# State-space scan kernel: the C row spread by fp32 transposes instead of bf16 parts, and two reorderings

## The reference, cut to what matters

```python
x_dbl = einsum('bkdl,kcd->bkcl', xs, x_proj_w)          # 8 dt rows, 16 B rows, 16 C rows
dts = softplus(einsum('bkrl,kdr->bkdl', dts, dt_projs_w) + dt_projs_b)
def step(h, inp):
    u, dt, Bl, Cl = inp
    dA = exp(dt[..., None] * A)
    h = h * dA + (dt * u)[..., None] * Bl[:, :, None, :]
    y = einsum('bkdn,bkn->bkd', h, Cl)
    return (h, y)
```

## Time and profile before

| | |
|---|---|
| median of 3 runs (lowest to highest) | 27172.97 us (27160.68 to 27182.06) |
| the profiled execution, its own time | 27187.59 us |
| its span in the trace | 27185.8 us |
| busy share of the span: DVE, ACT, POOL, PE | 93%, 87%, 86%, 80% |
| first layer and setup of the second (0 to about 3230 us) | not touched but for the setup |

### The profile page before, as it was taken

One profiled execution on the slowest core, in us unless ns is written; L12 is line 12 of the kernel. 1 busy time (PEld: TensorE's weight loads), 2 busy tenths in 40 slices (PEclk: granted clock), 3 DMA queues, 4 the chain that ended last, 5 costly groups with the idle time before them and its releaser, 6 DMA issues.

```text
span 27185.8 us, 494791 instructions
## 1 busy us (share of the span) xinstructions
PE 21719.7 (80%) x145198; PEld 16495.5 (61%) x145198; DVE 25255.5 (93%) x23743; ACT 23580.4 (87%) x48522; POOL 23338.1 (86%) x10372
## 2 busy tenths in 40 slices
PE   5888588888888888888888888888888888888887
PEld 1666366666666666666666666666666666666666
DVE  7777599999999999999999999999999999999999
ACT  2677499999999999999999999999999999999998
POOL 4000299999999999999999999999999999999999
PEclk6999799999999999999999999999999999999999
DMA  4111433333333333333333333333333333333333
GB/s 149 49 47 47 147 109 108 108 108 110 107 111 108 108 109 107 109 108 109 108 109 106 110 108 109 109 107 110 109 108 108 108 108 108 107 108 109 108 109 97
DMA packets 2189148, 2868.62 MB, mean 106 GB/s; under 512 B 695002, under 2 KB 964858, under 8 KB 2177786
## 3 DMA queue, kind: packets, MB, share of 16 engines
q1 hardware_dynamic: 2181978, 2803.33, 33.7%
q10 hardware_dynamic: 4608, 33.82, 0.3%
HBM read 2667.01 MB, written 169.74 MB: 104 GB/s over the span
## 4 chain that ended last, share of the span: by engine, by line
ACT 34%; PE 23%; issue 17%; DVE 11%; POOL 3%; ACTq 1%; DVEq 0%; POOLq 0%
DVE hst L1535 9%; ACT dbT L1424 8%; ACT dAs L1402 8%; PE yps L1240 7%; ACT dA L1402 6%; PE misc L1141 5%; PE dbx L1225 5%; ACT vab L1357 2%; PE misc L1177 2%; PE misc L1160 2%; POOL hc L1612 2%; DVE hc L1543 1%; ACT dbx L1402 1%; ACT vab L1343 1%; POOL dbu L1598 1%
## 5 line engine op out<-in xcount | busy, mean ns | idle before, releaser
L1598 POOL TENSOR_TENSOR dbu<-dtu,bb 128x1024 f32<-128x1024 f32 x4096 | 9699.4, 2375 | 867.0 <-DVE hst L1535 859.8
L1535 DVE TENSOR_TENSOR_SCAN hst<-dA,dbu 128x1024 f32<-128x1024 f32 x4096 | 9348.4, 2282 | 494.9 <-ACT dA L1402 417.8
L1612 POOL TENSOR_TENSOR hc<-hst,cc 128x1024 f32<-128x1024 f32 x4096 | 9734.0, 2376 | 4.9 <-DVE hst L1535 4.5
L1240 PE MATMUL yps<-ident,hc 128*128 128x128 f32 x65536 | 8781.6, 280 | 348.2 <-POOL hc L1612 343.5
L1240 PEld LDWEIGHTS yps<-ident,hc 128*128 128x128 f32 x65536 | 7809.8, 145 | 1479.9 <-issue 797.3
L1535 DVE TENSOR_TENSOR_SCAN hst<-dAs,dbx 128x1024 f32<-128x1024 f32 x3584 | 8118.4, 2265 | 102.2 <-ACT dAs L1402 51.7
L1225 PE MATMUL dbx<-ident,dbT 128*128 128x128 f32 x28672 | 4061.3, 287 | 3024.4 <-DVE hst L1535 2713.6
L1424 ACT ACTIVATE dbT<-dtuT,bT 128x256 f32<-128x256 f32 x14336 | 6124.6, 495 | 18.2
L1225 PEld LDWEIGHTS dbx<-ident,dbT 128*128 128x128 f32 x28672 | 3309.8, 146 | 4385.5 <-DVE hst L1535 3366.5
L1402 ACT ACTIVATE dA<-dtv,aneg 128x508 f32<-128x508 f32 x8192 | 5289.2, 678 | 371.6 <-DVE hst L1535 365.8
L1402 ACT ACTIVATE dAs<-dtv,aneg 128x508 f32<-128x508 f32 x7168 | 4741.1, 710 | 385.1 <-DVE hst L1535 385.0
(11 more groups left out here) (187 smaller groups left out, 25487.1 us busy)
## 6 DMA issues: line engine op xcount, KB each, us to landing
bb<-l_bscr SPq DMA_DIRECT2D x1024, 1024.0 KB, 5.7
cc<-l_bscr SPq DMA_DIRECT2D x1024, 1024.0 KB, 5.5
bx<-l_bscr SPq DMA_DIRECT2D x1024, 256.0 KB, 6.1
xg<-xgp SPq DMA_DIRECT2D x512, 85.0 KB, 2.3
xgp<-xb ACTq DMA_DIRECT2D x32, 1032.0 KB, 9.4
xt<-in_x_dram SPq DMA_DIRECT2D x128, 256.0 KB, 2.8
l_xnT<-xo SPq DMA_DIRECT2D x128, 256.0 KB, 2.0
xn<-l_xnT SPq DMA_DIRECT2D x256, 128.0 KB, 2.1
```

Of the source, the lines that this page charges most:

```text
L1240: mm = pe.matmul(yps[:, p, f * P:(f + 1) * P], hc[:, u % HB, f * 512 + p * P:f * 512 + (p + 1) * P], ident[:], is_transpose=True, start=fi ...
L1535: nc.vector.tensor_tensor_scan(hst[:, v % 4, way], decays.rearrange("p f c -> p (f c)")[:, way], inputs.rearrange("p f c -> p (f c)")[:, way],
L1598: nc.gpsimd.tensor_tensor(to, dtu[:, step % 2], row.unsqueeze(1).to_broadcast([P, 2, 512]), ALU.mult).then_inc(s_inp, 1)
L1612: nc.gpsimd.tensor_tensor(hc[:, v % HB].rearrange("p (f c) -> p f c", f=2), hst[:, v % 4].rearrange("p (f c) -> p f c", f=2), row.unsqueez ...
```

## The change

1. C by transposes. `side` with k = 0 turned the 128 rows of `xdbl` into columns already, for B. Now ACT copies the C columns as well (`bcT`, 32 columns in each of four positions of 128, before 16). `spread_c` makes four fp32 transposes, each of one column of `bcT` repeated 128 times, in place of one bf16 matmul. The casts (L1336, L1340), the matmuls of `split` (L1170), the constants `selc` and `nident` and the copies of the C rows in the projection's weights go. The x projection has 40 output rows in place of 104.
2. PE's order. In a step pair of DVE's kind the spread of C for u+2 now stands ahead of `total(u)`, also where it stood behind. Where POOL has the even product (u % 16 = 10), `total(u-1)` and `side` now stand ahead of the next `fill`. For u = 58 `total(u)` stays ahead of the spread, since no job stands at 58.
3. ACT's order. Decay 44 moves from the start of the pair u = 42 to right behind the Silus of u = 40, ahead of `scale(45)`.

The core of the diff:

```diff
-                        nc.scalar.copy(xdbl[0:104, j[2] % 2], misc[0:104, :])
-                        wait(act, s_cb, n * (NCD // 4) - NCD // 4)
-                        nc.scalar.copy(part[:, j[2] % 2], misc[0:96, :]).then_inc(s_me, 1)
-                    elif what == "split":
-
-                        r = 64 if j[3] == 1 else 32
-                        nc.scalar.copy(part[0:r, j[2] % 2], misc[0:r, :]).then_inc(s_me, 1)
+                        nc.scalar.copy(xdbl[0:DTR + 8, j[2] % 2], misc[0:DTR + 8, :]).then_inc(s_me, 1)
...
-                def spread_c(ph, u):
+                def spread_c(u):
 
                     step = u // NST
-                    if u % NST == 0:
-                        pe.wait_ge(s_me, ph.misc(("own" if step else "pre", "split", step, 2)))
-                    pe.matmul(cps[:, :], selc[:, u % NST], part[:, u // NST % 2], start=True, stop=True).then_inc(s_cb, 1)
+                    for p in range(4):
+                        mm = pe.transpose(cps[:, p * P:(p + 1) * P],
+                                          bcT[:, step % 2, p, u % NST:u % NST + 1].to_broadcast([P, P]), ident[:])
+                    mm.then_inc(s_cb, 1)
...
+                        if c_pool(u):
+                            total_odd()
+                            if ph.has(c):
+                                side(c[1], c[2], at(ph, c[0]))
+                            fill_next()
+                        else:
+                            fill_next()
+                            total_odd()
                             pe.wait_ge(s_hc, b * NCD + (c_dve_of(u) + 1))
-                        c = SIDE.get(u)
-                        if ph.has(c):
-                            side(c[1], c[2], at(ph, c[0]))
+                            if ph.has(c):
+                                side(c[1], c[2], at(ph, c[0]))
                         job_of(ph, u)
-                        early = ph.has(c) and u in JOBS
-                        if not early:
+                        if ph.has(c) and u not in JOBS:
                             total(u, b)
...
+                            spread_next()
+                        else:
+                            spread_next()
                             total(u, b)
...
                         if u + 2 < UN:
-                            decay(ph, u + 2, b)
+                            if u != SILU_AT + 2:
+                                decay(ph, u + 2, b)
...
                         if u == SILU_AT:
                             silus(ph, not last, True, b)
+                            decay(ph, u + 4, b)
```

More of the change, by code:

```diff
@@ L665, in layer1 @@
     UN = 4 * NST
+    DTR = 2 * NST
     HB = 4
@@ L709, in layer1 @@
         pbwd = sb("pbwd", [P, 2, P])
-        selc = sb("selc", [96, NST, P], BF16)
         wconv = sb("wconv", [P, 2, 9, P])
         wz = sb("wz", [P, 2, P])
-        wx = sb("wx", [P, 4, 2, 104])
-        wdt = sb("wdt", [104, 4, 2, P])
+        wx = sb("wx", [P, 4, 2, DTR + 8])
+        wdt = sb("wdt", [DTR + 8, 4, 2, P])
         wo = sb("wo", [P, 2, P])
@@ L743, in layer1 @@
         dtuT = sb("dtuT", [P, 2, 4, 256])
[L744 removed]
+        bcT = sb("bcT", [P, 2, 4, DTR])
         dbT = sb("dbT", [P, 2, 4, 256])
@@ L804, in _ @@
                         (pbwd[:], T["pbwd"].rearrange("o l q -> l o q")),
-                        (selF, T["selc"]),
                     ]
@@ L831, in _ @@
                     last.then_inc(s_scaled, 1)
-                    nc.vector.tensor_copy(selc[:], selF)
                     nc.vector.tensor_scalar(dtc[:], dtb[:], -1.0, 20.0, ALU.mult, ALU.add)
@@ L1159, in job @@
                         for f in range(2):
-                            mm = pe.matmul(misc[0:104, :], wx[:, KS[step], f], xs[:, KS[step] % 2, f],
+                            mm = pe.matmul(misc[0:DTR + 8, :], wx[:, KS[step], f], xs[:, KS[step] % 2, f],
                                            start=(f == 0), stop=(f == 1))
@@ L1265, in _ @@
                 pe.wait_ge(s_ce, 3)
-                spread_c(PRO, 0)
+                spread_c(0)
                 fill(1, 0)
@@ L1272, in body @@
                     for u in range(0, UN, 2):
-                        if turned(u + 3) and u + 3 < UN:
-                            fill(u + 3, b)
-                        elif u + 3 > UN and not last:
-                            fill(u + 3 - UN, b + 1)
-                        if u:
-                            total(u - 1, b)
-                        elif not (isinstance(b, int) and b == 0):
-                            total(UN - 1, b - 1)
-                        if not c_pool(u):
+                        c = SIDE.get(u)
@@ new lines, in fill_next, with total_odd @@
+                        def fill_next():
+                            if u + 3 > UN:
+                                if not last:
+                                    fill(u + 3 - UN, b + 1)
+                            elif turned(u + 3):
+                                fill(u + 3, b)
+                        def total_odd():
+                            if u:
+                                total(u - 1, b)
+                            elif not (isinstance(b, int) and b == 0):
+                                total(UN - 1, b - 1)
@@ new lines, in spread_next @@
+                        def spread_next():
+                            if ph.has(c):
+                                pe.wait_ge(s_ce, (at(ph, c[0]) * 4 + c[1]) * 3 + (c[2] + 1))
+                            if u + 2 < UN and not c_pool(u + 2):
+                                spread_c(u + 2)
+                            elif u + 2 == UN and not last:
+                                spread_c(0)
+                        if c_pool(u):
[6 more added lines that the diff above has]
+                            total_odd()
@@ L1289, in body @@
                             total(u, b)
-                        if ph.has(c):
-                            pe.wait_ge(s_ce, (at(ph, c[0]) * 4 + c[1]) * 3 + (c[2] + 1))
-                        if u + 2 < UN and not c_pool(u + 2):
-                            spread_c(ph, u + 2)
-                        elif u + 2 == UN and not last:
-                            spread_c(ph, 0)
-                        if early:
+                            spread_next()
+                        else:
+                            spread_next()
@@ L1411, in side @@
                     if k == 0:
-                        nc.scalar.copy(bT[:, step % 2], cps[:].rearrange("p (w n) -> p w n", w=4)[:, :, NST:2 * NST]).then_inc(s_ce, 1)
+                        nc.scalar.copy(bcT[:, step % 2], cps[:].rearrange("p (w n) -> p w n", w=4)[:, :, 0:DTR]).then_inc(s_ce, 1)
                     else:
@@ L1423, in scale @@
                     for p in blocks:
-                        last = nc.scalar.mul(dbT[:, turned_of(v) % 2, p], dtuT[:, step % 2, p], bT[:, step % 2, p, st:st + 1])
+                        last = nc.scalar.mul(dbT[:, turned_of(v) % 2, p], dtuT[:, step % 2, p], bcT[:, step % 2, p, NST + st:NST + st + 1])
                     if blocks[-1] == 3:
@@ L1685, in shape_constants @@
     pbwd = np.stack([np.ascontiguousarray(pfwd[:, o * P:(o + 1) * P].T) for o in range(2)])
-    selc = np.zeros((96, 16, P), np.float32)
-    for part in range(3):
-        for n in range(16):
-            selc[32 * part + n, n, :] = 1.0
     group = np.kron(np.eye(P // 4), np.full((4, 4), 0.25)).astype(np.float32)
-    return {"group": group, "ident": np.eye(P, dtype=np.float32), "pfwd": pfwd, "pbwd": pbwd, "selc": selc}
+    return {"group": group, "ident": np.eye(P, dtype=np.float32), "pfwd": pfwd, "pbwd": pbwd}
 def build(nc, given, out, N):
@@ L1698, in build @@
     second = {name[len("L1_conv_"):]: ap for name, ap in given.items() if name.startswith("L1_conv_")}
-    consts = {name: given[name] for name in ("ident", "group", "pfwd", "pbwd", "selc")}
+    consts = {name: given[name] for name in ("ident", "group", "pfwd", "pbwd")}
     layer0(nc, {**first, **consts, "l0_ln_w": first["ln_w"], "l0_ln_b": first["ln_b"], "x": given["x"], "x1T": x1T, "xgp": xgp}, N)
```

34 lines of the change are left out of this document (12 added, 22 removed).

## The result

The changed kernel takes 27276.53 us (median of 6 runs, 27273.56 to 27285.15). The kernel before takes 27175.58 us in its 6 runs, so the ratio is 1.0038, with an interval of 1.0028 to 1.0048. It is 0.38% slower, where 0.95% faster was forecast.

The account below looks back on a forecast made before the run. DVE and POOL, waiting for each other, were taken as the bound. Gains of 1.94 us per block times 127, 246 us, plus about 8 us in setup and prologue led to 26915 us, 0.95% faster; 8-in-10 range 26730 to 27070.

Parts of the forecast that it names:

- Steps 16 and 21: Product of step 16 and scan 21: earlier side copy and two fewer ACT casts gain 0.85 us per block together.
- Step 60: Product of step 60: total and side ahead of the fill end DVE's stall, leaving POOL's input 62 late; gain 0.55 us per block.
- Step 2: Product of step 2: its spread goes ahead of total 0 and decay 4 loses one cast; gain 0.25 us per block.
- Step 55: Softplus at step 55: ACT loses three casts between steps 49 and 52, so the vab waits go; gain 0.29 us per block.
- The Silu stall: DVE's 3.17 us wait at scan 44: cut up into waits at scan 44, scan 45 and the product of 44; gain 0.
- The rival that the stall really goes: At scan 44: the wait really disappears, gaining 1.0 us more per block, to POOL's limit, about 26790 us; chance 0.17.
- Spread: PE's four transposes replacing one matmul: +0.22 us each time, 28 times a block, 6.2 us of PE time.
- The sum: Whole kernel: gains of 1.94 us per block over 127 blocks, 246 us, plus about 8 us outside them; 26915 us.
- The setup's term: Setup and prologue: a load, a cast of selc, 16 small copies and first splits go; about 8 us gained, an estimate.
- PE's low clock: Rival, where PE has only transposes (step 55 to 0): low clock makes PE the bound, 27300 us; chance 0.04.
- the four terms of this forecast: Per-block gains: 0.85 us at steps 16 and 21, 0.55 at step 60, 0.25 at step 2, 0.29 at step 55.

## Why the prediction was wrong

**Steps 16 and 21 (forecast 0.85 us).** Right: 0.68 us in the changed kernel, and as much with the loads moved. Step 16 kept 0.60 us of its stall, not 0.3.

**Step 60 (forecast 0.55).** Right in kind, 0.70 us, and scan 62 now waits for POOL's input, as forecast:

```profile
14662.15 2.26 DVE L1534 TENSOR_TENSOR_SCAN hst<-dA,dbu 128x1024 f32<-128x1024 f32 x1
...
14668.12 2.29 DVE L1534 TENSOR_TENSOR_SCAN hst<-dA,dbu 128x1024 f32<-128x1024 f32 x1 [0.42 <-ACT dAs L1399]
```

```profile
14665.58 4.75 POOL L1597 TENSOR_TENSOR dbu<-dtu,bb 128x1024 f32<-128x1024 f32 x2
```

The view names `dAs` as what ended this wait (in 115 blocks), but scan 62 does not read `dAs`, and the program has it wait only for decay 62, which had ended 1.26 us earlier in the mean. POOL's input 62, the first of the two products in the row, ended 0.12 us ahead of scan 62 in each of blocks 4 to 123.

**What failed is the question behind this step.** Of the stall at 60 I asked who is late next among the engines, and stopped at POOL. I did not ask what else is timed by the same steps. SP sends the loads of the next block when POOL is through with its inputs, and that stands between the stall and the block's end. So the forecast put the block's start, scan 0 to 1, at nothing. Without the stall DVE reaches the branch 0.76 us sooner after these loads (scan 0 stands 6.35 us behind them in the mean of before, 5.59 now), and scan 1 comes 0.46 us later. The view of the earlier trace rows even had the sign of it, in a group of scans that I left out of my list of DVE's waits:

```profile
DVE hst L1535 <- issue: 49.3, 95, 1.0
```

It is now 101.8 us.

**Step 2 (forecast 0.25).** Wrong in the changed kernel, 0.35 us lost, and right with the loads moved, 0.32 gained. I had read this wait as one of PE's order, and it was one of PE's clock. In the kernel before (blocks 4 to 123) the clock falls in step 1 in 60 blocks, which are the half with the wait (4.72 us from scan 3 to 4); in the other 60 it falls just before the block begins, and the distance is 3.29 us, without a wait. In the changed kernel it falls in step 1 in 98.

**Step 55 (forecast 0.29).** 0.07 lost, and 0.33 gained with the loads moved. This term, too, named the wrong cause. In the kernel before the vab wait at step 55 is there in 60 blocks, exactly those in which PE's clock falls at step 54; without that fall the distance is 3.95 us. In the kernel with ACT's new order alone, which keeps every cast, the clock never falls at step 54 and the same 0.33 us are gained. In the changed kernel it still falls there in 50 blocks, which then take 4.92 us. The casts had no part in this wait. Where they do count is scan 21: 0.48 us there, and 0.50 with the spread alone.

**The Silu stall (forecast 0, bounds -0.1 and +1.0).** The mechanism was right to 0.01 us where PE kept its clock (27.61 us from scan 37 to the product of step 44, before 27.60). It left out that PE now waits for the scaling of step 45 behind decay 44 and is idle for 2.2 us, at which its clock falls in most blocks. That costs 0.34 us from scan 43 to 46 in the mean, outside my bound. The rival that the stall really goes is refuted.

**Spread (forecast +0.22 us each).** Right: four transposes of a repeated column take 0.60 to 0.65 us, 0.44 us apart. What it does beyond that I had not priced: at step 32 the decay is no longer in time (0.29 us), and the 18 instructions that its setup no longer has put DVE's loop where scan 32 stops for 0.36 us.

**The sum.** The setup's term (8 us) was about right. Scan 0 of the first block stands at 3225.7 instead of 3228.4, only 2.7 us earlier, but this holds the first layer too, which took 3.7 us longer in this execution. From the last reciprocal of the first layer (L597) to scan 0 it is 6.4 us less, and some 10 us less in the mean of the five profiles with the new spread and an unchanged setup against the five with the old one. From -1.94 us the steps lead to +0.82: scan 1 +0.46, step 4 0.60 worse than forecast, step 56 0.36 worse, step 32 +0.65, 43 to 48 +0.51, step 40 +0.16, steps 16 and 21 0.17 worse, step 60 0.15 better; together 2.76. 127 x 0.82 is 104 us, and the spans differ by 94. Moving the three loads gives 2.19 us back, 0.92 of them at scan 1, half of which is a stop that the kernel before had too. PE's low clock, which I had as a rival at 0.04, was the way in which more than half of the losses came: those at steps 4, 40, 43 to 48 and 56, together 1.63 of the 2.76 us, stand in the blocks where it falls. But it was not as that rival said: at 59, 60 and 63, where it fell 85, 41 and 66 times in before, it now falls 0, 0 and 3 times, although from step 57 to the block's end PE now has only transposes. It falls where PE has been idle, as the earlier trace rows had shown, though not after each idle stretch of that length.

Left open is why PE's clock holds at 54, and more often at 44, when loads at the block's start are moved, and what DVE waits for at scan 32.

## What to carry to other kernels

When a stall is removed, list what is released ahead of it and lands behind it: here DMA loads that had time to finish during the stall then ran into the loop's branch. Scans 1 and 4 lost 0.46 and 0.35 us, and the stall had given 0.70. Test a change with that neighbour moved as well, on the old kernel too: the change measured +0.38% with the loads where they were, and -0.8% with them moved. Read small groups of waits with no named cause, since such a one doubled here. And before a wait is put down to an engine's order or to a lost instruction, sort the blocks by the granted clock: two of the four terms of this forecast were waits of the clock.

## What the runs showed of the hardware

- After a loop's branch DVE stood still for up to 1.4 us where loads had been sent 5.6 us ahead of the last scan in front of it (the 16 DMA engines were 97.6% busy with data in the block shown), and not at all where they had been sent 7 us ahead or behind that scan. Moving three loads took 101.8 us of such waits to 0.6.
- 18 memsets more in a setup that runs once took 0.36 us from the distance between scans 31 and 32, in the mean of 120 blocks of a loop that they don't stand in.
- A transpose whose operand is one column repeated 128 times costs PE what a plain one does: four in 0.60 us at the clock of 1.00.
- Some 20 us with nothing but fp32 transposes on PE, from step 57 to the end of the changed kernel's block, left its granted clock at 1.00; it fell there in 3 of the 128 blocks.
- Eight matmuls of zeros (seven of them recorded, 1.67 us) in an idle stretch of 2.2 us kept PE's clock at its high level at step 44 in all 128 blocks (it fell in 46 with the loads moved and no such matmuls); ten of them at step 0, where with the loads moved PE had no long idle time, cost 0.77 us by scan 4.
